# Fourth attention: who forms the difference of the two softmaxes, and where it stands in VectorE's order

## The chip, the core and the metric

The kernel runs on one core of a Trainium2 chip. The core has five engines with an instruction stream each: TensorE (PE, matmuls and transposes), VectorE (DVE), ScalarE (ACT), GpSimd (POOL) and SyncE (SP, which starts DMAs). Each engine takes its instructions strictly as they are written; between engines there are semaphores. The metric is the device time of one execution in microseconds (us), here the median of several.

## The reference

Four blocks, each an attention and a feed forward with a residual and a layer norm, on 8 sequences of 256 tokens of width 256. The change is in the fourth attention, a differential one: 16 heads, each with two softmaxes over the same keys, and a third softmax over their difference.

```
energy = einsum('bqhad,bkhad->bahqk', qd, kd)          # a = 0, 1
energy = where(causal, NEG, energy)
scores = softmax(energy / sqrt(D), axis=-1)
lam    = exp(sum(lq1*lk1)) - exp(sum(lq2*lk2)) + LAM_INIT
diff   = scores[:, 0] - lam * scores[:, 1]
diff   = softmax(where(causal, NEG, diff), axis=-1)
att    = einsum('bhqv,bvhd->bqhd', diff, v)
att    = att * rsqrt(mean(att*att) + EPS) * rms_w * (1 - LAM_INIT)
return att.reshape(b, s, E) @ Wo
```

## The kernel before

Everything is written by hand, one stream per engine; nothing is scheduled by a tool. The fourth attention is `l3_attention`. A turn is one sequence of 256 tokens (a batch). It has eight slots, i = 0 to 7: four head rows r of four heads (g), and for each r both halves a. So an even slot computes the first softmax of four heads, an odd slot the second. All heads of a row are laid out as 128 query rows by 128 keys for the first query tile and by 256 keys for the second, which makes 384 columns per head.

The loop is software pipelined. In slot i the engines do this:

- TensorE: scores of slot i into four banks `S` (L1721, with the causal mask added, L1725); in odd slots the products with the values (`values`, L1748 and L1751); in even slots `turn_back` (L1760); then `turn`, the transposes (L1736) of two heads whose last softmax was made in the slot before; in slot 6 `turn_output` (L1767), in slot 7 the output projection (L1775), both of the batch before.
- VectorE: the first maxima of `S` (L1961); the maxima of the difference (L1989) and the bias made of them (L1991), for the two heads `part(i - 2)`; a copy of transposed weights out of the PSUM (L1997); `values_out` in odd slots (L2002), `take_output` in even ones (L2008, L2009); in slot 5 the norm of the batch before, in slot 7 its output and layer norm statistics; at the end of odd slots `ratios` (L1968 to L1970).
- ScalarE: the exponentials of slot i (L1864) with their row sums; a copy out of the PSUM (L1872); the second exponentials (L1881), which wait for the bias; in slot 6 a copy (L1887).
- GpSimd: for each r the mask on the first softmax (L1816), as soon as the even slot's exponentials are there; a share of the difference; in slot 4's time the squares of the attention output (L1833).

`S` is there once: the scores of slot i + 1 wait for the exponentials of slot i (`p_exp`), the exponentials for the first maxima (`nm_ready`), the maxima for the scores (`s_ps`).

The difference is made without dividing first. With `ratio` (row sum of a = 0 over that of a = 1, times minus lambda) it is `pr[a=0] + ratio * pr[a=1]`. Of the two heads of a part the even one is VectorE's, one SCALAR_TENSOR_TENSOR for each query tile (L1979), and the odd one GpSimd's, two multiplies by a broadcast ratio (L1826) and one add (L1829). VectorE makes the one for part 0 right behind the ratios, at the end of odd slots, and the one for part 1 just ahead of the second maxima, in even slots:

```
if live(i, 2, opening, closing):
    if i % 2 == 0:
        difference(b, i - 1)
    second_maxima(b, i)
...
if i % 2 == 1 and not closing:
    ratios(b, i)
    difference(b, i - 1)
```

The function `sequence` is written out for an opening batch, a middle one that runs in a loop and once more behind it, and a closing one with the two slots that the pipeline still owes.

## Time and profile before

| what | value |
|---|---|
| median of 3 runs | 3110.5 us (3109.22 to 3111.86) |
| the profiled execution, its own time | 3111.67 us |
| its span, first to last instruction | 3109.9 us |
| TensorE, VectorE, ScalarE, GpSimd busy, whole span | 84%, 60%, 42%, 12% |
| mean granted TensorE clock, whole span | 0.917 |
| L1864, first exponentials: busy, idle before | 207.1 us, 202.8 us |
| L1961, first maxima: busy, idle before | 124.6 us, 53.9 us |
| L1816, mask: busy, mean of one | 75.3 us, 2352 ns |

The profile is of one execution. Busy shares are averages over stages that have different limits, so they must be read stage by stage. The fourth attention lies between about 2117 us (first L1961) and 2604 us of the span. L1961, L1864 and the scores each wait for another of the three, which is the ring described above. In a timeline an idle time in brackets names what ended it. A row with "x4" stands for four neighbours of one line; its time is from the start of the first to the end of the last, and neighbours on VectorE overlap by about 0.08 us, so the start of the next row tells more than the length.

### The profile page before, as it was taken

The page shows a single profiled execution, that of the slowest core. Times are in us where ns is not written, and L with a number is a line of the kernel's source. Part 1 is how long each engine was busy: PE and PEld are TensorE (multiplying, and loading weights), DVE is VectorE, ACT ScalarE, POOL GpSimd, SP SyncE. Part 2 cuts the span into 40 slices and gives each one's busy share as a digit, 9 for nine tenths or more (in the row PEclk, how much of TensorE's full clock was granted, in tenths as well). Part 3 has the DMA queues.
Part 4 walks back from the last instruction along what each step waited for, and adds up shares of the span by engine and source line. Part 5 has one row for each costly group of instructions (what it writes and reads, how often), then busy time and mean ns, then how long its engine had stood idle before and what let it go on. Part 6 is the DMA issues. An engine that isn't in the chain of part 4 may idle for free. (4 is left out here: it accounts for less than half of the span.)

```text
span 3109.9 us, 43072 instructions
## 1 busy us (share of the span) xinstructions
PE 2608.6 (84%) x14256; PEld 1883.3 (61%) x14256; DVE 1858.5 (60%) x4295; ACT 1310.5 (42%) x3605; POOL 359.7 (12%) x392
## 2 busy tenths in 40 slices
PE   7988999889999999998698877796555654999997
PEld 5665544457776777677476665543443433877876
DVE  3665233445464555445645757546888886777777
ACT  4663455533443344334222132205777773332322
POOL 2440000000000000000121000003444440000000
PEclk9998999989999999999899888896777776999998
DMA  3002000000000000002000000100000003000000
GB/s 148 10 7 82 1 0 0 0 35 1 3 3 3 0 3 3 3 0 75 16 0 0 0 0 0 37 6 29 24 19 19 24 9 132 1 1 0 0 0 27
DMA packets 26415, 56.11 MB, mean 18 GB/s; under 512 B 3696, under 2 KB 22896, under 8 KB 24688
## 3 DMA queue, kind: packets, MB, share of 16 engines
q1 hardware_dynamic: 26352, 55.32, 4.8%
q8 instruction: 33, 0.54, 0.1%
q14 instruction: 30, 0.25, 0.0%
HBM read 39.59 MB, written 2.10 MB: 13 GB/s over the span
## 5 line engine op out<-in xcount | busy, mean ns | idle before, releaser
L1864 ACT ACTIVATE l3a_pr<-psum,l3a_nm 128x128 f32<-128x128 f32 (+1 forms) x512 | 207.1, 430 | 202.8 <-DVE l3a_nm L1961 202.8
L1721 PE MATMUL psum<-l3a_kr,l3a_qr 32*128 32x128 f32 (+1 forms) x1024 | 91.1, 491 | 180.3 <-ACT l3a_pr L1864 176.9
L108 DVE TENSOR_TENSOR x_sb<-psum,x_sb 128x512 f32 (+2 forms) x48 | 41.7, 868 | 235.2 <-PE psum L950 135.5
L757 DVE TENSOR_TENSOR l0f_hg<-l0f_sq,psum 128x512 f32<-128x512 f32 x128 | 87.8, 688 | 151.1 <-ACT l0f_sq L689 148.3
L1721 PEld LDWEIGHTS psum<-l3a_kr,l3a_qr 32*128 32x128 f32 x1024 | 51.5, 271 | 198.8 <-ACT l3a_pr L1864 186.3
L995 ACT ACTIVATE l1a_pr<-psum,l1a_nb,l1a_rq 128x128 f32<-128x128 f32 (+1 forms) x256 | 127.2, 509 | 87.2 <-DVE l1a_nb L1048 84.9
L1221 POOL TENSOR_TENSOR l1f_acc<-l1f_t 128x512 f32<-128x512 f32 x4 | 6.3, 1573 | 1334.3 <-DVE l1f_t L1284 1334.3
L2178 PE MATMUL psum<-l3f_x_hi,l3f_w_hi 128*128 x384 | 154.5, 402 | 6.6 <-DVE l3f_w_lo L2261 6.6
L2225 ACT ACTIVATE l3f_sg<-psum 128x512 f32<-128x512 f32 x96 | 57.3, 597 | 240.3 <-PE psum L2181 240.3
L1961 DVE TENSOR_REDUCE l3a_nm<-psum 128x2 f32<-128x256 f32 (+1 forms) x256 | 124.6, 548 | 53.9 <-PE psum L1725 53.9
L2179 PE MATMUL psum<-xT,l3f_w_hi 128*128 x384 | 152.9, 398 | 0.0
L2180 PE MATMUL psum<-l3f_x_hi,l3f_w_lo 128*128 x384 | 152.3, 397 | 0.0
L914 PE MATMUL psum<-l1a_kT,l1a_qT 128*128 128x128 f32 (+1 forms) x512 | 120.2, 359 | 20.9 <-ACT l1a_pr L995 14.0
L2192 PE MATMUL psum<-l3f_w_hi,l3f_h_hi 128*128 128x256 f32 x384 | 127.6, 332 | 7.9 <-DVE l3f_h_lo L2279 7.9
L1816 POOL TENSOR_TENSOR l3a_pr<-l3a_pr,w_l3a_mask 128x1024 f32<-128x1024 f32 x32 | 75.3, 2352 | 486.2 <-ACT l3a_pr L1864 486.2
L652 PE MATMUL psum<-l0f_hg,w_l0f_w 128*128 128x512 f32 x256 | 130.6, 593 | 0.8 <-DVE l0f_hg L757 0.8
L645 PE MATMUL psum<-l0f_xl,w_l0f_w 128*128 x256 | 130.6, 592 | 0.0
L1881 ACT ACTIVATE l3a_pr<-l3a_pr,l3a_nb,l3a_rec 128x128 f32<-128x128 f32 (+1 forms) x256 | 120.8, 581 | 3.8 <-DVE l3a_nb L1991 3.8
L885 PE MATMUL psum<-l1a_xc,w_l1a_q 128*128 128x256 f32 x512 | 122.4, 382 | 0.0
L687 ACT ACTIVATE l0f_relu<-psum 128x512 f32<-128x512 f32 x128 | 76.3, 596 | 108.8 <-PE psum L645 104.4
L867 PE MATMUL psum<-w_l1a_k,l1a_xc 128*128 128x512 f32 x256 | 112.8, 599 | 9.8 <-DMA l1a_xc<-xT 9.8
L891 PE MATMUL psum<-w_l1a_v,l1a_xc 128*128 128x512 f32 x256 | 120.3, 592 | 0.0
(424 smaller groups left out, 6942.2 us busy)
## 6 DMA issues: line engine op xcount, KB each, us to landing
w_l3f_all<-l3f_all_dram SPq DMA_DIRECT2D x1, 9216.0 KB, 25.7
l3a_qr<-l3a_q_all SPq DMA_DIRECT2D x32, 256.0 KB, 2.5
w_l0f_w<-l0f_w_dram SPq DMA_DIRECT2D x2, 2048.0 KB, 10.0
w_l1f_all<-l1f_all_dram SPq DMA_DIRECT2D x1, 2560.0 KB, 8.8
x_sb<-x_dram SPq DMA_DIRECT2D x1, 2048.0 KB, 8.5
l0a_xc<-xT SPq DMA_DIRECT2D x8, 256.0 KB, 2.5
w_l1a_q<-l1a_q_dram SPq DMA_DIRECT2D x1, 2048.0 KB, 7.9
w_l1a_k<-l1a_k_dram SPq DMA_DIRECT2D x1, 2048.0 KB, 13.5
```

What stands on the lines that cost most here:

```text
L645: mm(HB[e % 3], w["w1"][:, e, :], xl[:, chunk], start=True, stop=True).then_inc(h_ps, 1)
L652: mm(YL, w["w2"][:, e, :], hg[:, e % 2, :], start=(e == 0), stop=(e == E - 1)).then_inc(used, 1)
L885: last = mm(bank(2 + j % 2)[:, i * T:(i + 1) * T], w["q"][:, k, (2 * j + i) * HD:(2 * j + i + 1) * HD], xc[:, k, :], start=(k == 0), stop= ...
L995: last = nc.scalar.activation(pr[:, n % 2, i, s], S[n % 2][:, i, s], ACT.Exp, bias=nb[:, n % 2, t, i:i + 1], scale=rq[:, t, 2 * n + i:2 * ...
L1721: mm(S[:, g, t * P:t * P + (t + 1) * P], qr[rows, a, r, t * P:(t + 1) * P], kr[rows, a, 0:(t + 1) * P], start=(t == 0), stop=False, tile_p ...
L1864: last = nc.scalar.activation(pr[:, r, a, g, k], S[:, g, k], ACT.Exp, bias=nm[:, i % 2, g, t:t + 1], accum_out=sums[:, r, a, g, t:t + 1])
L1881: last = nc.scalar.activation(pr[:, r, 1, g, k], pr[:, r, 0, g, k], ACT.Exp, bias=nb2[:, r, g, t:t + 1], scale=rec[:, r, 0, g, t:t + 1])
L1961: last = nc.vector.tensor_reduce(nm[:, i % 2, 2 * pair:2 * pair + 2, t], S[:, 2 * pair:2 * pair + 2, t * P:t * P + (t + 1) * P], AX.X, ALU ...
L2178: mm(bk[e % 2], hi, x_hi[:, k, chunk], start=(k == 0), stop=False)
L2179: mm(bk[e % 2], hi, x_lo[:, k, chunk], start=False, stop=False)
L2180: mm(bk[e % 2], lo, x_hi[:, k, chunk], start=False, stop=(k == KD - 1))
L2192: mm(Y[:, t, :], h_hi[:, e % 2, tokens], hi, start=False, stop=False)
```

## The change

GpSimd keeps the mask and the squares and loses its share of the difference. VectorE forms the difference of both heads of a part, four SCALAR_TENSOR_TENSOR, at the head of `second_maxima`. And the call of `second_maxima` moves: from directly behind the first maxima to behind the copy, `values_out` or `take_output`, the norm and the output of the slot. The ratios stay last in odd slots. The semaphores `scaled`, `dif_even` and `dif_odd` go, `dif_ready` comes.

```
 @block.gpsimd
-                def difference(b, i):
-                    s = b * NU + i
-                    r, g = i // 2, part(i).start + 1
-                    if i % 2 == 0:
-                        pool.wait_ge(ratio_ready, b * R + r + 1)
-                        pool.wait_ge(masked, b * R + r + 1)
-                    for t in range(TT):
-                        k = slice(t * P, t * P + (t + 1) * P)
-                        last = nc.gpsimd.tensor_tensor(pr[:, r, 1, g, k], pr[:, r, 1, g, k], ratio[:, r, g, t:t + 1].broadcast_to((P, (t + 1) * P)), ALU.mult)
-                    last.then_inc(scaled, 1)
-                    pool.wait_ge(scaled, s + 1)
-                    nc.gpsimd.tensor_tensor(pr[:, r, 0, g, :], pr[:, r, 0, g, :], pr[:, r, 1, g, :], ALU.add).then_inc(dif_odd, 1)
...
                 with pool.Fori(0, B - 1) as b:
-                    for i in range(NU):
-                        if i % 2 == 0:
-                            mask(b + 1, i // 2)
-                        difference(b + 1, i)
-                        if i == 2:
+                    for r in range(R):
+                        mask(b + 1, r)
+                        if r == 1:
                             squares(b)
...
 @block.vector
-                def difference(b, i):
...
                 def second_maxima(b, i):
                     s = b * NU + i - 2
                     r, heads = (i - 2) // 2 % R, part(i - 2)
-                    dve.wait_ge(dif_even, s + 1)
-                    dve.wait_ge(dif_odd, s + 1)
+                    if i % 2 == 0:
+                        dve.wait_ge(ratio_ready, b * R + (i - 2) // 2 + 1)
+                        dve.wait_ge(masked, b * R + (i - 2) // 2 + 1)
+                    for g in range(heads.start, heads.stop):
+                        for t in range(TT):
+                            k = slice(t * P, t * P + (t + 1) * P)
+                            last = nc.vector.scalar_tensor_tensor(pr[:, r, 0, g, k], pr[:, r, 1, g, k], ratio[:, r, g, t:t + 1], pr[:, r, 0, g, k],
+                                                                  ALU.mult, ALU.add)
+                    last.then_inc(dif_ready, 1)
+                    dve.wait_ge(dif_ready, s + 1)
                     for t in range(TT):
                         last = nc.vector.tensor_reduce(nm2[:, r, heads, t], ...)
...
                             maxima(b, i)
                             if i == 7:
                                 stage_next(b)
-                        if live(i, 2, opening, closing):
-                            if i % 2 == 0:
-                                difference(b, i - 1)
-                            second_maxima(b, i)
                         if live(i, 3, opening, closing):
                             ...
                             out_of_psum(b, i)
...
                                 measure(nc, st, x_sb, mv, b * TT - TT, TT, lw)
+                        if live(i, 2, opening, closing):
+                            second_maxima(b, i)
                         if i % 2 == 1 and not closing:
                             ratios(b, i)
-                            difference(b, i - 1)
```

Line numbers shift in the changed kernel: L1961 becomes L1942, L1979 L1962, L1989 L1967, L1991 L1969, L1997 L1975, L2002 L1980, L1968 L1949, L1816 L1814, L1833 L1818.

VectorE, an odd slot (slot 5 of the opening batch) up to the first maxima of slot 6, before. `l3a_nm` are maxima and `l3a_nb` the bias, `l3a_pr` the exponentials, `l3a_pt` transposed ones, `w_l3a_q` the buffer with the attention output and its squares:

```order
L1961 TENSOR_REDUCE l3a_nm<-psum 128x2 x4
L1989 TENSOR_REDUCE l3a_nm<-l3a_pr 128x2 x2
L1991 TENSOR_TENSOR l3a_nb<-l3a_nm,l3a_rec 128x4
L1997 COPY l3a_pt<-psum 128x384
L2002 COPY w_l3a_q<-psum 128x256
L1968 RECIPROCAL l3a_rec<-l3a_sums 128x16
L1969 TENSOR_TENSOR l3a_ratio<-l3a_sums,l3a_rec 128x8
L1970 TENSOR_TENSOR l3a_ratio<-l3a_ratio,l3a_nlam 128x8
L1979 SCALAR_TENSOR_TENSOR l3a_pr<-l3a_pr,l3a_ratio 128x128
L1979 SCALAR_TENSOR_TENSOR l3a_pr<-l3a_pr,l3a_ratio 128x256
```

The same slot with the change:

```order
L1942 TENSOR_REDUCE l3a_nm<-psum 128x2 x4
L1975 COPY l3a_pt<-psum 128x384
L1980 COPY w_l3a_q<-psum 128x256
L1962 SCALAR_TENSOR_TENSOR l3a_pr<-l3a_pr,l3a_ratio 128x128
L1962 SCALAR_TENSOR_TENSOR l3a_pr<-l3a_pr,l3a_ratio 128x256
L1962 SCALAR_TENSOR_TENSOR l3a_pr<-l3a_pr,l3a_ratio 128x128
L1962 SCALAR_TENSOR_TENSOR l3a_pr<-l3a_pr,l3a_ratio 128x256
L1967 TENSOR_REDUCE l3a_nm<-l3a_pr 128x2 x2
L1969 TENSOR_TENSOR l3a_nb<-l3a_nm,l3a_rec 128x4
L1949 RECIPROCAL l3a_rec<-l3a_sums 128x16
L1950 TENSOR_TENSOR l3a_ratio<-l3a_sums,l3a_rec 128x8
L1951 TENSOR_TENSOR l3a_ratio<-l3a_ratio,l3a_nlam 128x8
```

The second maxima and bias moved from directly behind the first maxima to behind both copies, with four SCALAR_TENSOR_TENSOR ahead of them; the two behind the ratios are gone.

GpSimd, in the loop, from the mask of row 1 to the one of row 2, which is the next behind the last row shown, before:

```order
L1816 TENSOR_TENSOR l3a_pr<-l3a_pr,w_l3a_mask 128x4x2x128
L1822 REGISTER_ALU
L1826 TENSOR_TENSOR l3a_pr<-l3a_pr,l3a_ratio 128x128
L1826 TENSOR_TENSOR l3a_pr<-l3a_pr,l3a_ratio 128x256
L1829 TENSOR_TENSOR l3a_pr<-l3a_pr 128x384
L1832 ISA
L1833 TENSOR_TENSOR w_l3a_q<-w_l3a_q 128x512
L1826 TENSOR_TENSOR l3a_pr<-l3a_pr,l3a_ratio 128x128
L1826 TENSOR_TENSOR l3a_pr<-l3a_pr,l3a_ratio 128x256
L1828 REGISTER_ALU
L1829 TENSOR_TENSOR l3a_pr<-l3a_pr 128x384
```

With the change (the mask of row 2 is the last row):

```order
L1814 TENSOR_TENSOR l3a_pr<-l3a_pr,w_l3a_mask 128x4x2x128
L1817 ISA
L1818 TENSOR_TENSOR w_l3a_q<-w_l3a_q 128x512
L1813 REGISTER_ALU
L1814 TENSOR_TENSOR l3a_pr<-l3a_pr,w_l3a_mask 128x4x2x128
```

Six multiplies and adds around the squares are gone, so the mask of the next row follows the squares directly.

## Rows read from the trace of the kernel before

**Rows 1.** busy time in a stretch of one batch; columns as in its first line
```profile
core 0: us, PE busy (x) PEld busy (x) DVE busy (x) ACT busy (x) POOL busy (x), PEclk, DMA share, GB/s
...
2345.00:2403.00 58.00, 34.20 (x324) 23.03 (x324) 49.45 (x127) 44.00 (x169) 26.76 (x30) 0.76 0.06 20
```

**Rows 2.** timeline, VectorE: start, length, instruction, [idle before, releaser]
```profile
2336.70 1.95 DVE L1961 TENSOR_REDUCE l3a_nm<-psum 128x2 f32<-128x256 f32 x4 [1.27 <-PE psum L1725]
...
2345.33 1.94 DVE L1961 TENSOR_REDUCE l3a_nm<-psum 128x2 f32<-128x256 f32 x4
...
2352.00 1.95 DVE L1961 TENSOR_REDUCE l3a_nm<-psum 128x2 f32<-128x256 f32 x4 [1.14 <-PE psum L1725]
...
2355.33 0.56 DVE L1997 COPY l3a_pt<-psum 128x384 f32<-128x384 f32 x1 [0.27 <-PE psum L1736]
2355.80 0.41 DVE L2002 COPY w_l3a_q<-psum 128x256 f32<-128x256 f32 x1
2356.41 0.25 DVE L1968 RECIPROCAL l3a_rec<-l3a_sums 128x16 f32<-128x16 f32 x1 [0.19 <-ACT l3a_pr L1864]
...
2357.11 1.34 DVE L1979 SCALAR_TENSOR_TENSOR l3a_pr<-l3a_pr,l3a_ratio 128x128 f32<-128x128 f32 x2
2358.37 1.94 DVE L1961 TENSOR_REDUCE l3a_nm<-psum 128x2 f32<-128x256 f32 x4
2360.23 1.47 DVE L1979 SCALAR_TENSOR_TENSOR l3a_pr<-l3a_pr,l3a_ratio 128x128 f32<-128x128 f32 x2
...
2373.26 0.73 DVE L1979 SCALAR_TENSOR_TENSOR l3a_pr<-l3a_pr,l3a_ratio 128x128 f32<-128x128 f32 x2
2373.92 1.00 DVE L1989 TENSOR_REDUCE l3a_nm<-l3a_pr 128x2 f32<-128x256 f32 x2
2374.95 0.16 DVE L1991 TENSOR_TENSOR l3a_nb<-l3a_nm,l3a_rec 128x4 f32<-128x4 f32 x1
...
2375.54 0.20 DVE L2008 RECIPROCAL l3a_recs<-psum 128x8 f32<-128x8 f32 x1
...
2378.07 1.95 DVE L1961 TENSOR_REDUCE l3a_nm<-psum 128x2 f32<-128x256 f32 x4 [2.00 <-PE psum L1725]
...
2380.97 0.54 DVE L1991 TENSOR_TENSOR l3a_nb<-l3a_nm,l3a_rec 128x4 f32<-128x4 f32 x1
...
2382.24 0.67 DVE L2016 TENSOR_REDUCE l3a_vv<-w_l3a_q 128x32 f32<-128x512 f32 x1
...
2386.02 0.25 DVE L1968 RECIPROCAL l3a_rec<-l3a_sums 128x16 f32<-128x16 f32 x1
...
2387.97 1.93 DVE L1961 TENSOR_REDUCE l3a_nm<-psum 128x2 f32<-128x256 f32 x4
```

**Rows 3.** timeline, ScalarE, same columns
```profile
2356.60 1.89 ACT L1881 ACTIVATE l3a_pr<-l3a_pr,l3a_nb,l3a_rec 128x128 f32<-128x128 f32 x4
2359.42 0.37 ACT L1864 ACTIVATE l3a_pr<-psum,l3a_nm 128x128 f32<-128x128 f32 x1 [0.92 <-DVE l3a_nm L1961]
```

**Rows 4.** timeline, TensorE matmuls, same columns
```profile
2353.76 1.54 PE L1736 MATMUL psum<-cf_sb,l3a_pr 128*128 128x128 f32 x6
...
2358.55 0.87 PE L1736 MATMUL psum<-cf_sb,l3a_pr 128*128 128x128 f32 x6 [0.40 <-ACT l3a_pr L1881]
2362.79 1.67 PE L1721 MATMUL psum<-l3a_kr,l3a_qr 32*128 32x128 f32 x16 [3.37 <-ACT l3a_pr L1864]
```

**Rows 5.** timeline, GpSimd, same columns
```profile
2360.31 1.11 POOL L1829 TENSOR_TENSOR l3a_pr<-l3a_pr 128x384 f32<-128x384 f32 x1
2362.82 2.35 POOL L1816 TENSOR_TENSOR l3a_pr<-l3a_pr,w_l3a_mask 128x1024 f32<-128x1024 f32 x1 [1.40 <-ACT l3a_pr L1864]
...
2376.15 1.04 POOL L1833 TENSOR_TENSOR w_l3a_q<-w_l3a_q 128x512 f32<-128x512 f32 x1 [3.81 <-DVE w_l3a_q L2009]
...
2379.15 2.35 POOL L1816 TENSOR_TENSOR l3a_pr<-l3a_pr,w_l3a_mask 128x1024 f32<-128x1024 f32 x1
```

**Rows 6.** timeline, VectorE, end of this stage
```profile
2574.94 0.24 DVE L1968 RECIPROCAL l3a_rec<-l3a_sums 128x16 f32<-128x16 f32 x1
...
2586.38 0.56 DVE L1997 COPY l3a_pt<-psum 128x384 f32<-128x384 f32 x1 [1.73 <-PE psum L1736]
```

More of the change, by code:

```diff
@@ L1640, in l3_attention @@
         masked = sem("masked")
-        scaled = sem("scaled")
-        dif_even = sem("dif_even")
-        dif_odd = sem("dif_odd")
+        dif_ready = sem("dif_ready")
         nb_ready = sem("nb_ready")
@@ L1833, in squares @@
                     nc.gpsimd.tensor_tensor(osq[:, :, :], on[:, :, :], on[:, :, :], ALU.mult).then_inc(osq_ready, 1)
-                for i in range(NU):
-                    if i % 2 == 0:
-                        mask(0, i // 2)
-                    difference(0, i)
+                for r in range(R):
+                    mask(0, r)
                 with pool.Fori(0, B - 1) as b:
-                    for i in range(NU):
-                        if i % 2 == 0:
-                            mask(b + 1, i // 2)
-                        difference(b + 1, i)
-                        if i == 2:
+                    for r in range(R):
+                        mask(b + 1, r)
+                        if r == 1:
                             squares(b)
@@ L1970, in ratios @@
                     nc.vector.tensor_tensor(ratio[:, r, :, :], ratio[:, r, :, :], bc(by_quad[:, r, :], 2, TT), ALU.mult).then_inc(ratio_ready, 1)
-                def difference(b, i):
-                    r, g = i // 2 % R, part(i).start
-                    if i % 2 == 0:
-                        dve.wait_ge(ratio_ready, b * R + i // 2 + 1)
-                        dve.wait_ge(masked, b * R + i // 2 + 1)
-                    for t in range(TT):
-                        k = slice(t * P, t * P + (t + 1) * P)
-                        last = nc.vector.scalar_tensor_tensor(pr[:, r, 0, g, k], pr[:, r, 1, g, k], ratio[:, r, g, t:t + 1], pr[:, r, 0, g, k],
-                                                              ALU.mult, ALU.add)
-                    last.then_inc(dif_even, 1)
                 def second_maxima(b, i):
@@ L2033, in sequence @@
                                 stage_next(b)
-                        if live(i, 2, opening, closing):
-                            if i % 2 == 0:
-                                difference(b, i - 1)
-                            second_maxima(b, i)
                         if live(i, 3, opening, closing):
```

## The prediction

> **What bounds the kernel now.** I read the page first: TensorE is busiest over the whole span, but in the seven slices of the fourth attention VectorE and ScalarE fill most of their time and TensorE's granted clock falls. The one-batch stretch shows it: in 58.00 us VectorE is busy 49.45, ScalarE 44.00, TensorE 34.20, GpSimd 26.76 [rows 1]. Busy shares don't say what ends last, so I read the timeline of each engine over one batch.
>
> The marks are the first maxima (L1961), once per slot i = 0 to 7. The reader should see the distances in [rows 2]: 7 to 0 8.63, 0 to 1 6.67, 1 to 2 6.37, 5 to 6 9.90 us; slots 2 to 4 repeat the first two kinds within 0.01, 6 to 7 is like 0 to 1. The eight sum to 57.9. The ring is: maxima (VectorE), exponentials (ScalarE), next scores (TensorE), next maxima; the scores have only one set of banks. After an even slot the ring is bound by TensorE: the maxima wait 1.14 to 1.27 us for it, and VectorE has spare time. After an odd slot VectorE binds: ratios start as the exponentials end (2356.41), its difference (2357.11) stands directly ahead of the next maxima (2358.37), with no wait there. ScalarE enters slot 2's exponentials 0.92 us after it could [rows 3]; the second exponentials (1.89) are covered, because their bias (L1991) is ready early.
>
> **What the change does to VectorE's length.** Two things go from each pair of slots: the 1.26 us between L1979 and the next maxima, and a 1.40 us one after the maxima (1.47 busy, 2360.23). What comes are four L1979 in each slot. Their uncontended price is the row at 2373.26, when GpSimd had nothing left: 0.66 us from its start to the next instruction per pair, so 1.32 per slot, 2.64 per pair of slots. VectorE's sum therefore hardly changes: 2.66 out, 2.64 in. The long rows of before had GpSimd beside them: L1979 at 2360.23 ends only after GpSimd's add of 2360.31 plus 1.11 [rows 2, 5]. Of GpSimd's 26.76 us per batch four masks of 2.35 and the squares of 1.04 stay, 10.4; the 16 that go were off the path, except through that hold.
>
> **What it does to the order.** The whole of `second_maxima` now stands behind `out_of_psum`, `values_out`, `take_output`, the norms and the output. Its length is 1.32 + 1.19 (reduces and bias, 2373.92 to 2375.11) = 2.51 us. The ratios cost 0.70 (2356.41 to 2357.11). I follow a batch with times counted from the slot's maxima.
>
> *Odd slots 1 and 3.* The copy L1997 waits for the transposes of this slot, which end at 2355.30 [rows 4], 3.30 after the maxima; before, the second maxima filled that wait. Now: copy at 3.33, two copies 0.47 + 0.41 to 4.21, second maxima to 6.72, ratios to 7.42, next maxima. Before it was 6.37. TensorE can't hide it, ScalarE has the bias only at 6.72 rather than at about 3.1.
>
> *What follows in the even slot.* ScalarE's second exponentials run 1.89 from there, so TensorE's transposes for the even slot begin 1.30 after its maxima (before 0.18: 2358.55 against 2358.37), end at 2.17 at the full clock as in [rows 4], the copy takes 0.47, `take_output` about 0.55 (2375.54 to the squares it releases, 2376.15), the differences run 3.22 to 4.54, the reduces 1.03, and the bias multiply L1991 wants to start at 5.57. But GpSimd's mask starts 3.40 after the exponentials' start (2359.42 to 2362.82), and those start at 1.24, behind the second exponentials: the mask runs 4.64 to 6.99. In the trace L1991 beside the mask is held: 2380.97 plus 0.54 ends at 2381.51, the mask at 2381.50, where it otherwise takes 0.16 [rows 2, 5]. So the bias comes at 7.0, the next maxima at 7.0 rather than 6.67: plus 0.33. And ScalarE's second exponentials then end 1.9 after the odd slot's maxima, so its transposes start at 1.96 and end at 3.50 at the half clock (2353.76 took 1.54), 0.2 later than assumed above: the odd slot becomes 7.62, plus 1.25.
>
> The Trainium skill, "SBUF — State Buffer", section "Who interferes with whom", says that a VectorE instruction with two SBUF inputs and a GpSimd one that reads SBUF share one read port under an exclusive lock, and that a tensor_reduce never contends. By that rule the four differences, the bias multiply and nothing else can be held; the held rows agree, and the rule speaks against this change, since it puts both kinds of instruction into the mask's time.
>
> *Slot 4.* Here `take_output` also releases the squares (1.04 us) on GpSimd, at 3.2, just as the differences start; before they came after them. The second difference waits for the squares to 4.4, the third for the mask (4.64 to 6.99). Two differences, the reduces and the bias remain: 8.6 rather than 6.67, plus 1.93. If GpSimd yields instead, this is plus 0.3; I take the hold, since in every long row VectorE was the one held.
>
> *Slot 5.* Transposes start 2.0 after the maxima (ScalarE late), 0.87, two copies to 3.78, the norm 3.78 (2382.24 to 2386.02) to 7.56, second maxima to 10.07, ratios to 10.77: plus 0.87 on 9.90. At the half clock 0.67 more.
>
> *Slot 6.* As 0 and 2, with one more wait: `take_output` waits for the output transposes, now behind the late transposes. Plus 0.43.
>
> *Slot 7.* VectorE waited for the output projection anyway, so the 1.19 moved from ahead of it is not saved; 2.51 comes behind it, 1.26 of difference goes: plus 1.25, and 0.15 for a later projection: plus 1.40.
>
> Sum per batch: 2 x 0.33 + 2 x 1.25 + 1.93 + 0.87 + 0.43 + 1.40 = 7.8 us; seven such batches, 54.6. In the opening batch TensorE is the bound until slot 4; slots 4 to 7 are priced as an odd slot and a half, 2.3.
>
> *The end of the stage.* Two slots remain without first maxima. Before, their differences ran at once from the ratios at 2574.94, and the last copy that waits on their transposes started at 2586.38 [rows 6]. Now each second maxima stands behind the copy of the one before, so the two run one after the other: bias, 1.94 ScalarE, 1.60 transposes, 1.0 copies, 2.51, 7.05 each. From 2574.94 + 2.5 + 0.2, two of them give 2591.7, then 1.94 and 1.3: 2594.9. Plus 8.5, rounded down to 8.1 for faster transposes.
>
> Total 54.6 + 2.3 + 8.1 = 65.0. The profiled execution took 3111.67, so 3176.7; it lies 1.2 over the median of the runs, so 3175.5, given as **3175**. The feed forward behind is untouched.
>
> **Costed at nothing.** The self-wait for dif_ready: in the trace the reduces follow L1979 with no gap (2373.26, 2373.92). The masks earlier on GpSimd: they wait for the same exponentials. The later norm: `output` on ScalarE and the projection take it up within slot 6 and 7's sums.
>
> **Rivals.**
> - *Order alone (3145).* The holds don't fall where I put them (GpSimd waits, or the mask comes before or after). Then even slots stay at 6.67, odd ones get 1.05, slot 5 about 0.2, slot 7 1.25: 3.6 per batch, 25, with 1.7 and 7 for the ends: 34 on 3110.5. For it: the margins are half a microsecond. Against: L1991 would stand at 5.57, well inside the mask. 21 in 100.
> - *Differences fall under the mask too (3205).* If TensorE's granted clock is at the lower level (1.2 GHz) in the even slots, its transposes take 0.67 more (1.54 against 0.87), the fourth difference would start at 4.79, after the mask's start at 4.64, and be held to 7.2; reduces and bias put the next maxima at 8.4 instead of 7.0. In all of three slots of seven batches that is 29: 3205. For it: TensorE idles longer, and in the odd slot of [rows 4] the transposes took 1.54. Against: the level at these transposes was full in the batch shown. 18 in 100.
> - *Faster (3087).* The 1.26 ahead of the maxima leaves the path in slots 5 and 7 (17.6 in seven batches) and about 0.4 in slots 1 and 3 (5.6), since scores were ready sooner: 23 less. It decides if the new second maxima fit where VectorE idles, that is if the bias is ready before ScalarE finishes its exponentials, at 4.6. Against: in the odd slot the copy's wait alone reaches 3.33, and 3.4 of work follow. 3 in 100.
> - *No effect that shows (3110).* Full clock in the odd slots too (1 us earlier copies) and no holds: odd slots then come to about 6.5, the rest cancels. 4 in 100.
>
> My forecast keeps 54 in 100; its own range is 3158 to 3192, from the choice of clock in slots 1, 3 and 5 (0.67 x 3 x 7 = 14 either way). Measurements of this kernel tell no change from one of 0.2%, 6 us. Faster 3, within it 4, slower 93 in 100. The range 3138 to 3205 takes in order alone and nearly all of the clock rival.
>
> **What the new profile would show.** Right: maxima distances near 7.0 and 7.6 in turn, 8.6 after slot 4, 10.8 after 5, 10.0 after 7; L1991's successor at 1 us or more in even slots, ending with the mask; the copy in odd slots waiting over 1 us on the transposes; ScalarE waiting for the bias. Wrong: uncontended pairs that still take over 0.7, a bias at 5.7 in even slots, or copies in odd slots that don't wait. A granted clock far from 0.76 in this stage would move the sum either way.

## The result: 4.15% slower

The kernel after takes 3241.13 us (median of 4 runs, 3236.3 to 3242.34), the kernel before 3111.18 beside it (4 runs, 3109.22 to 3112.91). The ratio is 1.0415, 95% interval 1.0397 to 1.0433. The forecast of 3175 had the sign, but the time lies 36 us above the end of its range. The profiled execution took 3236.3 us (span 3234.5), so it is 124.6 over the 3111.67 of the one before.

The page of the profile after, its engines, its clock and the groups of the fourth attention (line, engine, operation, count | busy us, mean ns of one | idle before, releaser):

```profile
PE 2658.5 (82%) x14256; PEld 1915.0 (59%) x14256; DVE 1924.6 (60%) x4423; ACT 1312.5 (41%) x3605; POOL 234.7 (7%) x200
...
PEclk9998999899999999997999888966556555899999
...
L1845 ACT ACTIVATE l3a_pr<-psum,l3a_nm 128x128 f32<-128x128 f32 (+1 forms) x512 | 205.7, 418 | 102.4 <-DVE l3a_nm L1942 101.9
L1862 ACT ACTIVATE l3a_pr<-l3a_pr,l3a_nb,l3a_rec 128x128 f32<-128x128 f32 (+1 forms) x256 | 119.1, 535 | 224.7 <-DVE l3a_nb L1969 224.7
...
L1962 DVE SCALAR_TENSOR_TENSOR l3a_pr<-l3a_pr,l3a_ratio 128x128 f32<-128x128 f32 (+1 forms) x256 | 141.1, 613 | 0.0
L1814 POOL TENSOR_TENSOR l3a_pr<-l3a_pr,w_l3a_mask 128x1024 f32<-128x1024 f32 x32 | 80.2, 2506 | 833.6 <-ACT l3a_pr L1845 833.6
```

Lines of after used below, with those of before in brackets: L1942 first maxima (L1961), L1962 difference (L1979), L1967 second maxima (L1989), L1969 bias (L1991), L1975 copy (L1997), L1949 to L1951 ratios, L1845 first exponentials (L1864), L1862 second exponentials (L1881), L1868 ScalarE's copy of the output (L1887), L1734 transposes (L1736), L1746 values (L1748), L1773 output projection (L1775), L1719 scores (L1721), L1814 mask (L1816), L1818 squares (L1833).

The reader is to see that ScalarE now waits 224.7 us for the bias, in front of the second exponentials, where it waited 3.8 us before. That is the new wait. Some 100 us of it take the place of the wait for the first maxima, which fell from 202.8 to 102.4, so the two together grew by 120.5 us. VectorE's share stays at 60% and GpSimd falls from 12% to 7%: no engine got fuller. A row that answers to [rows 1], batch 4 of after in a window of its own length:

```profile
core 0: us, PE busy (x) PEld busy (x) DVE busy (x) ACT busy (x) POOL busy (x), PEclk, DMA share, GB/s
...
2398.30:2473.20 74.90, 43.12 (x324) 28.84 (x324) 58.28 (x142) 44.13 (x170) 11.27 (x5) 0.54 0.05 16
```

It is the same work in 74.90 us as in 58.00 before. ScalarE is busy for as long as before (44.13 against 44.00). TensorE is busy for longer (43.12 against 34.20), at a granted clock of 0.54, nearly always at the lower of its two levels (1.2 and 2.4 GHz), where it was 0.76.

The distances between first maxima, as means of batches 1 to 7 (slot 7: six of them), worked out from the timelines; the forecast is that of the prediction added to the mean of before:

| slot | 0 | 1 | 2 | 3 | 4 | 5 | 6 | 7 | sum |
|---|---|---|---|---|---|---|---|---|---|
| before | 6.67 | 6.42 | 6.65 | 6.46 | 6.55 | 10.01 | 6.66 | 8.79 | 58.2 |
| forecast | 7.00 | 7.67 | 6.98 | 7.71 | 8.48 | 10.88 | 7.09 | 10.19 | 66.0 |
| after | 7.46 | 7.57 | 8.15 | 7.50 | 9.06 | 11.26 | 8.98 | 14.16 | 74.1 |

Where the 124.6 us are: 106.3 in these distances (504.9 against 398.6), 4.4 in the opening batch, 12.7 from the last slot 7 to the end of the stage (47.0 against 34.3), 2.2 ahead of the stage, and -0.9 behind it. The 2.2 are no effect of the change: over all fourteen profiles of this document the stage's first maxima lie between 2113.1 and 2118.9.

VectorE over batch 4 of after, to be set beside [rows 2] (start, length, instruction, idle before and releaser):

```profile
2398.30 1.95 DVE L1942 TENSOR_REDUCE l3a_nm<-psum 128x2 f32<-128x256 f32 x4 [0.35 <-issue]
...
2404.28 1.15 DVE L1969 TENSOR_TENSOR l3a_nb<-l3a_nm,l3a_rec 128x4 f32<-128x4 f32 x1
2405.35 1.94 DVE L1942 TENSOR_REDUCE l3a_nm<-psum 128x2 f32<-128x256 f32 x4
2408.95 0.56 DVE L1975 COPY l3a_pt<-psum 128x384 f32<-128x384 f32 x1 [1.67 <-PE psum L1734]
...
2409.76 1.40 DVE L1962 SCALAR_TENSOR_TENSOR l3a_pr<-l3a_pr,l3a_ratio 128x128 f32<-128x128 f32 x4
...
2412.92 1.95 DVE L1942 TENSOR_REDUCE l3a_nm<-psum 128x2 f32<-128x256 f32 x4
2415.93 0.56 DVE L1975 COPY l3a_pt<-psum 128x384 f32<-128x384 f32 x1 [1.05 <-PE psum L1734]
...
2416.84 3.49 DVE L1962 SCALAR_TENSOR_TENSOR l3a_pr<-l3a_pr,l3a_ratio 128x128 f32<-128x128 f32 x4
2420.36 1.01 DVE L1967 TENSOR_REDUCE l3a_nm<-l3a_pr 128x2 f32<-128x256 f32 x2
...
2433.06 4.27 DVE L1962 SCALAR_TENSOR_TENSOR l3a_pr<-l3a_pr,l3a_ratio 128x128 f32<-128x128 f32 x4
```

GpSimd in the same batch, beside [rows 5]:

```profile
2402.77 2.64 POOL L1814 TENSOR_TENSOR l3a_pr<-l3a_pr,w_l3a_mask 128x1024 f32<-128x1024 f32 x1 [20.44 <-ACT l3a_pr L1845]
2417.57 2.47 POOL L1814 TENSOR_TENSOR l3a_pr<-l3a_pr,w_l3a_mask 128x1024 f32<-128x1024 f32 x1 [12.17 <-ACT l3a_pr L1845]
2433.22 1.08 POOL L1818 TENSOR_TENSOR w_l3a_q<-w_l3a_q 128x512 f32<-128x512 f32 x1 [13.18 <-DVE w_l3a_q L1987]
2434.26 2.52 POOL L1814 TENSOR_TENSOR l3a_pr<-l3a_pr,w_l3a_mask 128x1024 f32<-128x1024 f32 x1
```

Four differences take 1.40 us where GpSimd is idle (2409.76), 3.49 where the mask starts 0.73 after them (2417.57), 4.27 where squares and mask both fall on them (2433.22, 2434.26). In slot 0 the mask takes only the bias, which then takes 1.15 rather than 0.16. The maxima of the difference (L1967), with one SBUF input each, take 1.01 at 2420.36 as elsewhere. All of that is as forecast; that the differences of slot 2 are under the mask is not. The cause is on TensorE, beside [rows 4]:

```profile
2414.35 1.54 PE L1734 MATMUL psum<-cf_sb,l3a_pr 128*128 128x128 f32 x6 [0.71 <-ACT l3a_pr L1862]
...
2461.51 1.08 PE L1746 MATMUL psum<-l3a_pt,w_l3a_k 128*32 128x256 f32 x8 [4.41 <-ACT w_l3a_q L1868]
...
2462.95 1.54 PE L1734 MATMUL psum<-cf_sb,l3a_pr 128*128 128x128 f32 x6
2464.29 3.06 PE L1773 MATMUL psum<-l3a_wo,w_l3a_q 128*128 128x256 f32 x8
```

The transposes of the even slot take 1.54, at the lower level, where [rows 4] had 0.87 for them. And the last three rows are slot 7, with a wait that the prediction had left out: the products with the values wait 4.41 us for ScalarE's copy of the output.

### The profile page after: what moved, and what is told of

Its sections match the earlier page's. It is cut to its first block and busy times, and to the rows that moved or that the text cites. A ratio compares the mean times of both kernels' runs of the same rounds, so it can differ in the third digit from the quotient of the medians.

```text
span 3234.5 us, 42850 instructions
## 1 busy us (share of the span) xinstructions
PE 2658.5 (82%) x14256; PEld 1915.0 (59%) x14256; DVE 1924.6 (60%) x4423; ACT 1312.5 (41%) x3605; POOL 234.7 (7%) x200
## 5 line engine op out<-in xcount | busy, mean ns | idle before, releaser
L1845 ACT ACTIVATE l3a_pr<-psum,l3a_nm 128x128 f32<-128x128 f32 (+1 forms) x512 | 205.7, 418 | 102.4 <-DVE l3a_nm L1942 101.9
L1862 ACT ACTIVATE l3a_pr<-l3a_pr,l3a_nb,l3a_rec 128x128 f32<-128x128 f32 (+1 forms) x256 | 119.1, 535 | 224.7 <-DVE l3a_nb L1969 224.7
L1734 PE MATMUL psum<-cf_sb,l3a_pr 128*128 128x128 f32 x384 | 93.4, 411 | 126.9 <-ACT l3a_pr L1862 126.5
L1719 PE MATMUL psum<-l3a_kr,l3a_qr 32*128 32x128 f32 (+1 forms) x1024 | 97.8, 523 | 108.8 <-ACT l3a_pr L1845 105.6
L1734 PEld LDWEIGHTS psum<-cf_sb,l3a_pr 128*128 128x128 f32 x384 | 69.3, 212 | 150.9 <-ACT l3a_pr L1862 148.2
L1962 DVE SCALAR_TENSOR_TENSOR l3a_pr<-l3a_pr,l3a_ratio 128x128 f32<-128x128 f32 (+1 forms) x256 | 141.1, 613 | 0.0
L1814 POOL TENSOR_TENSOR l3a_pr<-l3a_pr,w_l3a_mask 128x1024 f32<-128x1024 f32 x32 | 80.2, 2506 | 833.6 <-ACT l3a_pr L1845 833.6
L914 PE MATMUL psum<-l1a_kT,l1a_qT 128*128 128x128 f32 (+1 forms) x512 | 120.6, 360 | 20.9 <-ACT l1a_pr L995 14.0
L1942 DVE TENSOR_REDUCE l3a_nm<-psum 128x2 f32<-128x256 f32 (+1 forms) x256 | 124.7, 549 | 15.5 <-PE psum L1723 13.6
L1719 PEld LDWEIGHTS psum<-l3a_kr,l3a_qr 32*128 32x128 f32 x1024 | 55.6, 292 | 132.0 <-ACT l3a_pr L1845 116.8
```

The costliest lines, as they stand in the source:

```text
L1719: mm(S[:, g, t * P:t * P + (t + 1) * P], qr[rows, a, r, t * P:(t + 1) * P], kr[rows, a, 0:(t + 1) * P], start=(t == 0), stop=False, tile_p ...
L1734: last = nc.tensor.transpose(PT[j][:, k * P:(k + 1) * P], pr[:, r, 1, heads.start + j, k * P:(k + 1) * P], c["id"])
L1845: last = nc.scalar.activation(pr[:, r, a, g, k], S[:, g, k], ACT.Exp, bias=nm[:, i % 2, g, t:t + 1], accum_out=sums[:, r, a, g, t:t + 1])
L1942: last = nc.vector.tensor_reduce(nm[:, i % 2, 2 * pair:2 * pair + 2, t], S[:, 2 * pair:2 * pair + 2, t * P:t * P + (t + 1) * P], AX.X, ALU ...
L1962: last = nc.vector.scalar_tensor_tensor(pr[:, r, 0, g, k], pr[:, r, 1, g, k], ratio[:, r, g, t:t + 1], pr[:, r, 0, g, k], ALU.mult, ALU.add)
```

## The experiments

Ratios are to the kernel before on the same chip, with 95% intervals. Theory A is that of the prediction: the late place of the second maxima and the holds beside GpSimd's work. Its rivals were the order alone, the clock, VectorE's larger share, and the output copy on ScalarE.

### split_only: the new division, the old order

```
+                        if live(i, 2, opening, closing):
+                            second_maxima(b, i)       # directly behind the first maxima
 ...
-                        if live(i, 2, opening, closing):
-                            second_maxima(b, i)       # behind the measure
```

> VectorE forms all differences as in the changed kernel, but second_maxima (differences, reduces, bias) stands where it stood before, directly behind the first maxima. Theory A (the place in the order is the cause, VectorE's larger share is nearly free): the bias is ready 4.4 us after the maxima, as the exponentials end and the mask starts; odd slots 5.96 to 6.67 against 6.37, slot 5 9.75 against 9.90, slot 7 8.5 against 8.66: 3095 to 3115 us. Rival B (the share itself, 1.32 us of differences a slot, is the cost): each slot about 1.3 longer in part, over 3150 us.

Measured: 3105.07 us (10 runs, 3098.7 to 3113.9), ratio 0.9983 [0.9973, 0.9992]. The expectation held for the time. Slots 1 and 3 have 5.83 and 6.33 and slot 7 8.70, near what was expected, but slot 5 has 10.06 and not 9.75. VectorE in an even slot of it:

```profile
2451.85 1.95 DVE L1942 TENSOR_REDUCE l3a_nm<-psum 128x2 f32<-128x256 f32 x4 [0.34 <-issue]
2453.72 1.40 DVE L1962 SCALAR_TENSOR_TENSOR l3a_pr<-l3a_pr,l3a_ratio 128x128 f32<-128x128 f32 x4
2455.15 1.01 DVE L1967 TENSOR_REDUCE l3a_nm<-l3a_pr 128x2 f32<-128x256 f32 x2
2456.19 0.16 DVE L1969 TENSOR_TENSOR l3a_nb<-l3a_nm,l3a_rec 128x4 f32<-128x4 f32 x1
```

The mask starts at 2456.32, as the bias ends: nothing is held. So at the old place it costs nothing that VectorE does all the differences; the loss comes with the late place of the second maxima.

### order_only: the new order, the old division

```
-                        if live(i, 2, opening, closing):
-                            if i % 2 == 0:
-                                difference(b, i - 1)
-                            second_maxima(b, i)
 ...                                                   # behind the measure:
+                        if live(i, 2, opening, closing):
+                            if i % 2 == 0:
+                                difference(b, i - 1)
+                            second_maxima(b, i)
```

> The split of the difference between VectorE and GpSimd of the kernel before is kept; only the second maxima (and VectorE's difference for the second part) move behind the copies, norm and output, as in the changed kernel. Theory A (order): bias of even slots at about 4.9 us, in the mask, so held to 7; odd slots 7.4 to 7.6; slot 7 long as in the changed kernel; differences themselves seldom under the mask: 3180 to 3230 us. Rival B (the share): under 3130 us.

Measured: 3165.94 (3162.03 to 3166.97), ratio 1.0173 [1.0156, 1.019], below the expected band. Slots 0, 2, 4 and 6 have 6.69, 6.73, 6.51 and 6.74, close to before, slots 1, 3 and 5 have 7.30, 7.35 and 11.01, and slot 7 has 13.56. GpSimd and VectorE in its slot 0 (batch 4), where mask and bias start within 0.01 us of each other:

```profile
2371.30 2.34 POOL L1816 TENSOR_TENSOR l3a_pr<-l3a_pr,w_l3a_mask 128x1024 f32<-128x1024 f32 x1 [1.50 <-ACT l3a_pr L1864]
```

```profile
2371.31 2.35 DVE L1991 TENSOR_TENSOR l3a_nb<-l3a_nm,l3a_rec 128x4 f32<-128x4 f32 x1
```

GpSimd in its slot 4 (batch 3):

```profile
2334.78 0.99 POOL L1829 TENSOR_TENSOR l3a_pr<-l3a_pr 128x384 f32<-128x384 f32 x1
2335.73 2.37 POOL L1816 TENSOR_TENSOR l3a_pr<-l3a_pr,w_l3a_mask 128x1024 f32<-128x1024 f32 x1
```

The bias is held here too: for 2.35 us in the batch shown, in 16 of the 21 slots 0, 2 and 6 of batches 1 to 7 by the mask, and in slot 4 by GpSimd's add (there the bias starts at 2334.83 and takes 0.96). Even so slot 0 takes only 6.73 in that batch against 6.66. What the old division spares are the differences: VectorE has two of them behind the copies of an even slot instead of four, and they are through before the mask starts. So the late place costs 55 us with the old division (over 3111) and 136 with the new one (3241 over split_only's 3105): most of the loss comes from the two halves of the change together. Slot 7 is long all the same, and its values wait 2.38 us for ScalarE's copy of the output (2421.74).

### thin_mask: hardly any mask

```
-                    nc.gpsimd.tensor_tensor(diagonal, diagonal, bc(bc(w["mask"], 1, 2), 1, G), ALU.add)...
+                    nc.gpsimd.tensor_tensor(diagonal[:, 0, 0, 0:8], diagonal[:, 0, 0, 0:8], w["mask"][:, 0:8], ALU.add)...
```

> The changed kernel, but GpSimd adds the mask to 8 columns instead of 1024 (the causal mask on the first softmax is left out apart from these). Theory (the mask holds VectorE's differences and bias): slots 0, 2, 4, 6 lose 0.4, 1.6, 2.3 and 1.9 us, slot 7 about 2 because the output copy on ScalarE comes earlier: some 8 a batch, 3183 us, less if TensorE's clock rises as well. Rival (the late order alone, the holds hide under it): within 10 us of 3241.

Measured: 3178.58, ratio 1.0221 [1.0204, 1.0238]. 62.6 us below after: the price of the mask's holds, from a kernel whose VectorE does all that after's does. Slots 2, 4 and 6 fall to 6.88, 6.94 and 6.89, about as expected. Slot 7 was expected to lose about 2 and stays at 14.01.

### copy_first: the output copy ahead of the second exponentials

```
-                        if live(i, 2, opening, closing):
-                            second(b, i)
                         if i == 6 and not opening:
                             output(b - 1)
+                        if live(i, 2, opening, closing):
+                            second(b, i)
```

> The changed kernel, but in slot 6 ScalarE makes the output copy (L1868) ahead of the second exponentials instead of behind them. Theory (in slot 7 TensorE's products with the values wait for that copy, which waits for the bias held by the mask): TensorE's slot 7 starts 2 to 3 us earlier as far as the transposes allow, 2 us a batch: 3227 us. Rival (TensorE is bound by the transposes' own wait for the second exponentials): no change, 3241 within 4.

Measured: 3215.71 (3215.21 to 3216.16), ratio 1.0337 [1.032, 1.0354]; 25.4 below after, more than expected. Slot 7 goes from 14.16 to 12.41 and slot 2 from 8.15 to 7.61. That the copy is late costs time, and it isn't all: slot 7 stays 2.2 above its forecast. TensorE's transposes there now wait for the second exponentials, whose bias is held, and are still at 1.54:

```profile
2450.44 1.54 PE L1734 MATMUL psum<-cf_sb,l3a_pr 128*128 128x128 f32 x6 [2.29 <-ACT l3a_pr L1862]
```

### late_even and late_odd: the late place in one kind of slot

```
+                        if i % 2 == 1 and live(i, 2, opening, closing):
+                            second_maxima(b, i)       # early
 ...
+                        if i % 2 == 0 and live(i, 2, opening, closing):
+                            second_maxima(b, i)       # late; late_odd has the two parities exchanged
```

> The changed kernel, with second_maxima behind the copies in even slots only; in odd slots it stands directly behind the first maxima as before. Theory (the mask and the squares hold VectorE's work in even slots; slot 7 pays for the late output copy of slot 6): slots 0, 2 near 6.9, slot 4 near 8.4, odd slots 5.8 to 6.7, slot 7 near 11.5: about 3150 us. Rival (the wait of odd slots on the transposes is what costs): near 3110.

> The changed kernel, with second_maxima behind the copies in odd slots only. Then the bias of even slots comes at 4.4 us, ahead of the mask, and nothing is held. Theory (each parity costs by its own mechanism): slots 1 and 3 near 7.4, slot 5 10.5, slot 7 9.9, even ones 6.7: 4 a batch and some 4 at the end, 3140 us. Rival (only the hold costs): near 3105 as with the old place.

Measured: late_even 3153.07, ratio 1.0135 [1.0118, 1.0152]; late_odd 3141.1, ratio 1.0099 [1.0082, 1.0116]. Both times are as expected, but not every slot. In late_odd slots 1 and 3 take 6.69 and 6.75 and not 7.4: their transposes take 0.9 there in six of seven batches, the full level. In late_even they take 6.94 and 7.07, above the 5.8 to 6.7. Over split_only the two cost 48 and 36 us, 84 together; both at once (after) cost 136. The 52 us between are an interaction: late even slots alone leave slots 0 and 2 at 6.76 and 6.79, where after has 7.46 and 8.15, because in late_even the last difference starts 3.7 to 4.3 us after the maxima and the mask at 4.5. In slots 0 and 2 the differences fall under the mask only when the odd slot before was late too. Slot 7 has 11.59 and 10.29 with one kind late, 14.16 with both.

### fill_before and fill_after: matmuls of zeros to raise the clock

```
+                        if i in (0, 2, 4) and not closing:     # behind turn(b, i)
+                            for _ in range(8):                 # 6 in fill_after
+                                mm(OT, c["zero"], bc(c["idb"], 1, 4), start=True, stop=True)
```

> The kernel before, with 8 extra matmuls of zeros (512 columns) behind the transposes in slots 0, 2 and 4, into a bank that is free then, while TensorE waits for exponentials. Theory C (the granted clock of the scores in slots 1, 3, 5 is set by the idle time ahead of them): those scores take 0.94 instead of 1.66 us, even slots fall from 6.66 to about 5.7, 3 a batch: 3090 us. Rival (the granted clock doesn't follow, or other waits take over): 3105 to 3120.

> The changed kernel with 6 such extra matmuls at the same place. Theory C (the clock stays at the lower level for want of work on TensorE and with it the transposes of even slots come 0.67 later, which puts the fourth difference under the mask): slots 2, 4, 6 lose up to 1.6, 0.8 and 1.9, slot 5 0.6, slot 7 about 1.5: 5 a batch, 3205 us. Rival (the clock is a symptom, the holds stay): 3235 to 3250.

Measured: fill_before 3105.88 (10 runs, 3104.65 to 3107.1), ratio 0.9985 [0.9976, 0.9995], where I had expected 3090: its rival was right, by its second half. The scores of slots 3 and 5 do fall to 0.94, from 1.66 in nearly every batch, but those of slot 1 stay at 1.66, and those of slot 2 rise from 0.94 to 1.6. fill_after 3227.58 (3222.79 to 3230.49), ratio 1.0378 [1.0361, 1.0396], where I had expected 3205 and the rival at least 3235: it lies between them. The granted clock over 2300 to 2500 us is 0.76 before and 0.78 in fill_before. Of after and of fill_after these are the rows of that stretch (same columns as above):

```profile
2300.00:2500.00 200.00, 110.45 (x868) 74.17 (x868) 156.39 (x384) 121.39 (x465) 30.18 (x13) 0.60 0.04 15
```

```profile
2300.00:2500.00 200.00, 117.84 (x984) 76.12 (x984) 159.44 (x387) 122.24 (x466) 33.93 (x15) 0.71 0.05 16
```

In fill_before slots 2 and 4 fall to 5.74 and 5.73, but slots 5 and 7 rise by 0.8 each, and slot 1 by 0.2, and give nearly all of it back: a batch sums to 58.1 against 58.2. Of the 6.7 us between the two profiles 3.2 lie in the opening batch. In fill_after the clock rises from 0.60 to 0.71 and the distances hardly move (slot 2 from 8.15 to 7.63, slot 7 to 13.95): the transposes of the even slots stand ahead of the filler, and most of them still take 1.54 (in slots 0, 2, 4 and 6 of batches 1 to 7, 21 of 28). A higher mean clock is worth what the instructions on the path get of it.

### mask_late and mask_late_copy: the same work without the holds

In mask_late GpSimd's mask waits until VectorE's bias is written, and the squares until that of slot 4:

```
                     pool.wait_ge(p_exp, b * NU + 2 * r + 1)
+                    if not (isinstance(b, int) and b == 0 and r == 0):
+                        pool.wait_ge(nb_ready, b * NU + 2 * r - 1)
 ...
                     pool.wait_ge(on_raw, b * R + R)
+                    pool.wait_ge(nb_ready, b * NU + NU + 3 if not isinstance(b, int) else b * NU + NU)
```

> The changed kernel; GpSimd's mask also waits for the bias of its even slot, and the squares for that of slot 4, so that neither can run beside VectorE's differences or bias. The same work as in the changed kernel. Theory (it is the holding, not GpSimd's work): even slots fall to 6.7 to 6.9 as with the thin mask, 3178 us. Rival (with the thin mask less work was the gain, a later mask makes the next second maxima or the squares late): over 3220.

Measured: 3182.56 (3180.66 to 3184.22), ratio 1.0234 [1.0217, 1.0251], as expected. 58.6 us below after, though nothing is left out: that is the price of the holds, by a second way beside thin_mask. The distances are 6.69, 7.18, 6.87, 7.15, 6.87, 10.80, 6.89 and 14.01.

mask_late_copy adds copy_first's edit to it.

> As mask_late, and ScalarE's output copy of slot 6 ahead of its second exponentials. Theory (what is left in slot 7 is TensorE's products with the values waiting for that copy, then transposes and projection in line): slot 7 falls from about 13.8 to 12, 13 us in all: 3165. Rival (slot 7 is then bound by the transposes' wait): 3178.

Measured: 3144.04 (3143.19 to 3147.31), ratio 1.0112 [1.0095, 1.0129]. The edit brings 38.5 us here, not the 13 expected: three times as much. TensorE in slot 7 of mask_late:

```profile
2356.63 1.08 PE L1746 MATMUL psum<-l3a_pt,w_l3a_k 128*32 128x256 f32 x8 [2.31 <-ACT w_l3a_q L1871]
...
2358.07 1.54 PE L1734 MATMUL psum<-cf_sb,l3a_pr 128*128 128x128 f32 x6
2359.41 3.44 PE L1773 MATMUL psum<-l3a_wo,w_l3a_q 128*128 128x256 f32 x8
```

The same place in mask_late_copy:

```profile
2343.84 1.08 PE L1746 MATMUL psum<-l3a_pt,w_l3a_k 128*32 128x256 f32 x8
...
2345.56 0.88 PE L1734 MATMUL psum<-cf_sb,l3a_pr 128*128 128x128 f32 x6 [0.21 <-ACT l3a_pr L1865]
2346.27 1.89 PE L1773 MATMUL psum<-l3a_wo,w_l3a_q 128*128 128x256 f32 x8
```

With the 2.31 us of waiting goes the lower clock level: transposes 0.88 instead of 1.54, projection 1.89 instead of 3.44. Slot 7 falls to 10.46, close to its forecast of 10.2. That also tells why the same edit brought only 1.75 us in slot 7 of after: there the transposes stayed at 1.54 and the projection took 3.62. Slot 7 makes 21 of the 38.5 us. Another 9.5 lie in slots 1, 3, 4 and 5, and in slots 1 and 3 it is again the level: their transposes take 0.9 in six of seven batches, where mask_late has 1.1 to 1.5. So the edit's worth is only in part the wait that it takes away.

### fill_split and fill_split_mask: a version that beats both

fill_split is split_only with the eight matmuls of fill_before. fill_split_mask moves the squares behind the mask of the next part too:

```
                         mask(b + 1, r)
-                        if r == 1:
+                        if r == 2:
                             squares(b)
```

> VectorE forms all differences with second_maxima at its old place, and 8 extra matmuls of zeros behind the transposes of slots 0, 2 and 4. Theory: the early differences leave room (odd slots 5.8), so that faster scores in even slots come through where they can: 3090 us. Rival: as in the kernel before with the filler, slots 5 and 7 give it back: 3100 to 3108.

> fill_split, with GpSimd's mask of row 2 ahead of the squares instead of behind them. In fill_split that mask runs from the end of slot 4 to 2.2 us into slot 5 and holds the differences there (2.47 us for the four instead of 1.40). Theory: the mask then starts at 4.5 of slot 4, the squares end near 2.1 of slot 5 and hold them by 0.3 at most; slot 5 falls from 10.7 to about 9.9, 5 us in all: 3084. Rival (slot 5 is bound elsewhere): 3089.

Measured: fill_split 3089.13 (3087.36 to 3092.07), ratio 0.9933 [0.9916, 0.995]; fill_split_mask 3083.79 (5 runs, 3083.39 to 3089.24), ratio 0.992 [0.9907, 0.9934]. Both as expected, and the two fastest of all. The runs of the two overlap, and the two profiled executions took the same time (3087.3 and 3087.1): batches 1 to 7 are 5.2 us shorter in the second, and what stands behind them is 4.5 us longer. So their times alone don't tell them apart; slot 5 does, 10.69 against 9.63. VectorE there in fill_split, whose squares and mask (2363.35 to 2365.70) fall on the difference:

```profile
2364.43 2.47 DVE L1965 SCALAR_TENSOR_TENSOR l3a_pr<-l3a_pr,l3a_ratio 128x128 f32<-128x128 f32 x4
```

And in fill_split_mask, where the mask ran from 2358.79 and the squares from 2361.11:

```profile
2361.93 1.42 DVE L1965 SCALAR_TENSOR_TENSOR l3a_pr<-l3a_pr,l3a_ratio 128x128 f32<-128x128 f32 x4
```

The filler brings 16 us here by the medians (3105.07 to 3089.13) and 5 in fill_before. By the distances the difference is mostly in slot 7, which fill_before lengthens from 8.79 to 9.55 and fill_split leaves at 8.73 (8.70 in split_only); slot 5 gets longer in both, from 10.01 to 10.82 and from 10.06 to 10.69. The profiles show only 9.6 of the 16 us, since the profiled execution of split_only was the fastest of its ten.

## Why the prediction was wrong

**What held.** VectorE's length: four differences 1.40 with no gap before the reduces, and split_only shows that the division is free. The late bias as the mechanism: ScalarE's 224.7 us. Odd slots 1 and 3: plus 1.25 forecast, plus 1.15 and 1.04 measured, with a copy that waits 1.67 in slot 1; the half clock that the forecast took for them is in the rows of slot 1 in every batch and of slot 3 in three of seven. The hold of the bias in slot 0. The doubt in slot 4, whether GpSimd yields: VectorE was held there too (4.27), and GpSimd's own mask grew from 2.35 to at most 2.64. The Trainium skill, "SBUF — State Buffer", section "Who interferes with whom", gives a lock that whoever issues first keeps for its whole instruction. The rows agree: one by one, the fourth difference of slot 2 is issued at 2417.76, after the mask's start at 2417.57, and ends at 2420.33, after the mask's end at 2420.05; L1967 was never held. The end of the stage, less well: 9.5 forecast with the last slot 7, 12.7 measured.

**The step that failed first: the clock of the even slot's transposes.** The prediction let them "end at 2.17 at the full clock as in [rows 4]", against the rival with "the level at these transposes was full in the batch shown". But the batch shown was of before, with a granted clock of 0.76; in after it is 0.54, and the transposes take 1.54 in slots 0 and 6 of all seven batches and in slot 2 of five. In slot 2 they start 1.43 us after the maxima in batches 1 to 6, whatever their length. At 1.54 they end at 2.97, the fourth difference starts at 4.84, behind the mask's start at 4.65, and it and with it all of the second maxima are held. At 0.88 they end at 2.31 and the fourth difference starts at 4.18, ahead of the mask. Batch 5 of after happens to have the full level in slot 2. TensorE, then VectorE there:

```profile
2489.28 0.88 PE L1734 MATMUL psum<-cf_sb,l3a_pr 128*128 128x128 f32 x6 [2.04 <-ACT l3a_pr L1862]
```

```profile
2487.85 1.95 DVE L1942 TENSOR_REDUCE l3a_nm<-psum 128x2 f32<-128x256 f32 x4
...
2491.11 1.39 DVE L1962 SCALAR_TENSOR_TENSOR l3a_pr<-l3a_pr,l3a_ratio 128x128 f32<-128x128 f32 x4
...
2493.58 1.30 DVE L1969 TENSOR_TENSOR l3a_nb<-l3a_nm,l3a_rec 128x4 f32<-128x4 f32 x1
```

The mask starts at 2492.51, the differences are just past, only the bias is held (1.30), the next maxima start at 2494.80, and the distance is 6.95: the forecast's 7.0. So it is in batches 1 and 5; in the other five, with transposes of 1.54, slot 2 takes 8.6 to 8.8, the 8.4 of the rival "Differences fall under the mask too".

In slot 0 the lower level alone isn't enough. There the transposes start at 1.01 and end at 2.55 in batches 2 to 6, the fourth difference starts at 4.42, just ahead of the mask at 4.47, and the slot takes 7.05 or less; only in batches 1 and 7, where they end at 2.77 and 2.88, does it take 8.39 and 8.62. Slot 6 takes 8.98 every time: the differences also wait for the output transposes and start at 4.31 (2454.16), which is the 0.4 that the prediction had for that wait, and then they are held. No batch has the full level there, so how much of it is the clock's isn't shown.

Over slots 0, 2 and 6 this is 24.6 us in seven batches above the forecast, 13.2 of them in slot 6 and 8.2 in slot 2, and 6.7 more in slots 4 and 5. Slot 5 takes 10.68 in batch 5, with transposes of 0.87, and 11.3 to 11.4 in the other six, with 1.54: the 0.67 that the prediction named for the half clock. The rival was the right mechanism at 18 in 100; it should have been the forecast, with a margin to the mask of a few tenths and, in its own words, "TensorE idles longer".

**The second step that failed: slot 7, "0.15 for a later projection".** I followed VectorE and not TensorE's queue. Ahead of its values in slot 7 stands

```
 if i == 7 and not opening: pe.wait_ge(oT_ready, b)
 values(b, i)
```

and oT_ready is signalled by ScalarE's copy of the output, which stands behind the second exponentials of slot 6, and these now wait for a held bias. ScalarE in batch 4 of after:

```profile
2458.93 1.86 ACT L1862 ACTIVATE l3a_pr<-l3a_pr,l3a_nb,l3a_rec 128x128 f32<-128x128 f32 x4 [4.12 <-DVE l3a_nb L1969]
2460.70 0.57 ACT L1868 ACTIVATE w_l3a_q<-psum 128x512 f32<-128x512 f32 x1
```

The first maxima of slot 7 are at 2458.83. The copy ends 2.4 after them, and values, transposes and projection line up behind it in TensorE's queue. That the bias is late is enough, it needn't be held: thin_mask and mask_late, in which nothing holds it, have slot 7 at 14.01, with values that wait 2.31 for the copy. VectorE in that slot of after:

```profile
2458.83 1.95 DVE L1942 TENSOR_REDUCE l3a_nm<-psum 128x2 f32<-128x256 f32 x4
...
2464.53 0.56 DVE L1975 COPY l3a_pt<-psum 128x384 f32<-128x384 f32 x1 [3.42 <-PE psum L1734]
...
2467.51 0.69 DVE L108 TENSOR_TENSOR x_sb<-psum,x_sb 128x512 f32 x1 [2.09 <-PE psum L1773]
```

The output comes 8.68 us after the maxima. In batch 4 of before, it is 4.55. VectorE:

```profile
2394.63 1.95 DVE L1961 TENSOR_REDUCE l3a_nm<-psum 128x2 f32<-128x256 f32 x4 [1.28 <-PE psum L1725]
...
2399.18 0.69 DVE L108 TENSOR_TENSOR x_sb<-psum,x_sb 128x512 f32 x1 [0.31 <-PE psum L1775]
```

TensorE, batch 4 of before:

```profile
2395.18 1.08 PE L1748 MATMUL psum<-l3a_pt,w_l3a_k 128*32 128x256 f32 x8 [0.16 <-issue]
...
2396.40 0.87 PE L1736 MATMUL psum<-cf_sb,l3a_pr 128*128 128x128 f32 x6
2397.11 1.89 PE L1775 MATMUL psum<-l3a_wo,w_l3a_q 128*128 128x256 f32 x8
```

The 4.13 between them: values start 2.13 later (2.68 against 0.55 after the maxima), transposes take 0.67 more, the projection 1.17 more; the rest, 0.16, is in the values' second half and the starts. With the 1.25 of second maxima behind it, that is 5.38. The mean over six batches is plus 5.37, where 1.40 was forecast, 24 us in all; batch 4 itself has 5.7, so that the two numbers are so close is chance. The copy had nothing to do with it in before, where it ran at 2394.31 and ended 0.3 us after the maxima. mask_late_copy takes the wait away and has slot 7 at 10.46.

**The sum, from kernels.** From split_only at 3105: the late place without holds 77 (mask_late), of which the output copy is 38.5 (mask_late_copy); the holds by mask and squares 58.6 more. The pieces depend on each other: taken out of after alone, the copy is worth 25.4 (copy_first). The forecast had 65 for all, 34 of it for the order alone and so 31 for the holds. What fell out was the copy and nearly half of the holds. mask_late_copy, which is order alone with the copy out of the way, has 34 over before (3144.04 against 3110.22), the number of the rival "Order alone", but in part by luck: slots 1 and 3 were priced at 1.05 more and have 0.23 and 0.38, since their transposes are at the full level, while slot 5 has 0.61 for 0.2, slot 7 1.67 for 1.25, and slots 2 and 6 have 0.2 where nothing was forecast.

**What stays open.** What decides the level at which the even slots' transposes run. fill_after raises the mean clock and most of them still take 1.54. In mask_late those of slot 2 take 0.88 in six of seven batches; in mask_late_copy, in which TensorE waits less in slot 7, they take 1.54 in six of seven. So that a wait more on TensorE brings the lower level isn't shown slot by slot, only in the mean (0.54 against 0.76). And copy_first is 25 us faster than after; in the two profiles it is 20.9, of which 13.6 lie in the distances of batches 1 to 7, 3.6 ahead of the stage, where the edit does nothing, and 3.6 behind the last first maxima. I didn't trace these last.

## What to carry to other kernels

When an instruction group moves later on one engine, follow every queue that its result releases to the end of the iteration, also those in which something else stands behind the waiting instruction: here the copy of the output, unrelated to the moved work, cost 25.4 us, and 38.5 with the holds out of the way. Where a margin to a contending instruction is a few tenths of a microsecond, price the case on both clock levels, and give the lower one a good chance if the change makes TensorE wait more. To give VectorE work that has two SBUF inputs was free here where GpSimd wasn't reading SBUF meanwhile: at the old place the new division is -0.2% (split_only against before), at the late place it is +2.4% (3241.13 against order_only's 3165.94).

## What the runs showed of the hardware

- A tiny instruction pays the whole hold: the bias, 4 columns per partition, takes 0.16 us, but 1.15 and 1.30 where it came while the mask ran (after), and 2.35 where it started 0.01 us behind the mask (order_only, 2371.31).
- Both sides wait, at very different prices: VectorE's four differences went from 1.40 to 3.49 and 4.27, GpSimd's mask only from 2.35 to at most 2.64. The difference under way when the mask starts takes 0.3 to 0.5 us by itself, the mask 2.35.
- TensorE's busy share hides its clock: 43.12 us busy of 74.90 at 0.54 in after, 34.20 of 58.00 at 0.76 in before. The share is 0.58 and 0.59, since the lower level makes the same work longer.
- Eight matmuls of zeros in each of slots 0, 2 and 4 gained 16 us on split_only, although they are pure additional work for TensorE.
